# A graph-attention stage whose loads are all issued before its first group is released

## The reference, cut to what matters

```python
x = x + _L0_gnn_ref(_layernorm(x), adj, W, a)        # attention:  e = leaky_relu(s1 + s2); e = where(adj > 0, e, NEG)
                                                     #             elu(softmax(e) @ h), h = x @ W
x = x + _L0_ffn_ref(_layernorm(x), Wg, bg, W1, ...)  # 8 experts, the best two of each row, hidden size 512
x = x + _L1_gnn_ref(_layernorm(x), adj, ...)         # three steps of a GRU, each over the graph's edges
x = x + _L1_ffn_ref(_layernorm(x), gate_w, ...)      # 16 experts, the best two of each row, hidden size 256
```

## Time and profile before

| | us |
|---|---|
| median of 3 runs (1354.57 to 1358.33) | 1354.96 |
| the profiled execution, its own time | 1351.87 |
| span of its trace | 1350.0 |
| attention stage, to the first load of the experts | 274.3 |
| PE / DVE / POOL / ACT busy, whole span | 1025.9 / 797.4 / 623.2 / 563.3 |

### The profile page before, as it was taken

The page is one execution under the profiler, slowest core; times in us unless marked ns, Lnnn a source line. Parts: engine busy times, 40 slices in busy tenths (PEclk is TensorE's granted clock), DMA queues, the critical chain, the costliest instruction groups (busy, mean ns, idle before and its releaser), DMA issues. The chain is left out here.

```text
span 1350.0 us, 27968 instructions
## 1 busy us (share of the span) xinstructions
PE 1025.9 (76%) x6752; PEld 825.6 (61%) x6753; DVE 797.4 (59%) x3187; ACT 563.3 (42%) x1364; POOL 623.2 (46%) x686
## 2 busy tenths in 40 slices
PE   3666656379999999289988977979851989989930
PEld 3555445279999999245545544645430989988930
DVE  4776777445555555347767957768552444434418
ACT  3555555233333333146545644545430333333315
POOL 3577677724444554301335244253354355555540
PEclk8666666589999999789989989989965999999975
DMA  4223231222222221222203112040004322222229
GB/s 119 63 80 88 74 97 38 69 66 70 66 67 64 68 66 53 59 63 63 72 23 91 41 57 86 8 132 12 20 32 90 77 73 81 73 76 76 65 82 322
DMA packets 126205, 98.73 MB, mean 73 GB/s; under 512 B 33864, under 2 KB 115400, under 8 KB 126152
## 3 DMA queue, kind: packets, MB, share of 16 engines
q1 hardware_dynamic: 105536, 61.24, 16.7%
q0 software_dynamic: 17152, 35.29, 7.9%
q10 hardware_dynamic: 3464, 1.59, 0.6%
HBM read 55.44 MB, written 42.62 MB: 73 GB/s over the span
## 5 line engine op out<-in xcount | busy, mean ns | idle before, releaser
L1433 POOL DMA_INDIRECT result<-e_y,e_ids x280 | 274.6, 981 | 278.8 <-DVE e_y L1547 115.0
L1462 PE MATMUL e_ps_h<-e_xT,e_up_of 128*128 128x128 f32 x2240 | 290.1, 280 | 24.7 <-issue 21.8
L1462 PEld LDWEIGHTS e_ps_h<-e_xT,e_up_of 128*128 128x128 f32 x2240 | 271.4, 195 | 32.6 <-issue 29.6
L1477 PE MATMUL e_ps_y<-w_sb,e_hT 128*128 x1664 | 214.1, 278 | 5.5 <-issue 3.3
L1477 PEld LDWEIGHTS e_ps_y<-w_sb,e_hT 128*128 128x128 f32 x1664 | 200.7, 194 | 6.6 <-issue 6.2
L375 POOL DMA_INDIRECT queue<-g_q_rows,g_q_slots x128 | 129.8, 1014 | 77.9 <-DVE g_q_gap L320 38.4
L375 POOL DMA_INDIRECT queue<-a_r_rows,a_r_slots x128 | 129.0, 1008 | 63.9 <-issue 44.2
L1501 ACT ACTIVATE e_hT<-e_ps_h,b_sb 128x128 f32<-128x128 f32 x272 | 78.3, 377 | 139.6 <-remote 93.5
L1540 DVE TENSOR_SCALAR e_hT<-e_ps_h,b_sb 128x128 f32<-128x128 f32 x272 | 76.5, 343 | 84.6 <-remote 78.2
L1529 DVE COPY e_up_of<-w_sb 128x512 f32 x280 | 109.1, 430 | 5.5 <-issue 3.2
L1556 DVE TENSOR_TENSOR e_hT<-e_ps_h,e_gate 128x512 f32<-128x512 f32 x72 | 49.6, 689 | 101.7 <-ACT e_gate L1510 66.9
(11 more groups left out here) (218 smaller groups left out, 1892.4 us busy)
## 6 DMA issues: line engine op xcount, KB each, us to landing
e_xq<-queue SPq DMA_DIRECT2D x280, 64.5 KB
g_y<-result SPq DMA_DIRECT2D x16, 512.0 KB
o_y<-result SPq DMA_DIRECT2D x16, 512.0 KB, 5.3
w_sb<-w SPq DMA_DIRECT2D x48, 128.0 KB
result<-e_y,e_ids POOLq DMA_INDIRECT x280
x_res<-x SPq DMA_DIRECT2D x16, 256.0 KB
w_sb<-w SPq DMA_DIRECT2D x16, 256.0 KB
out<-x_res SPq DMA_DIRECT2D x16, 256.0 KB, 4.6
```

The costliest lines, as they stand in the source:

```text
L1433: pool.indirect_dma_start(out=result, out_offset=bass.IndirectOffsetOnAxis(ap=ids[at_down.k][:, t, :].bitcast(U32), axis=0), in_=y[at_down ...
L1462: last = pe.matmul(ps_h[b][:, t, q * P:(q + 1) * P], up_of[at_up.k % 4][:, t, q * P:(q + 1) * P], xT[at_up.k % 4][:, t, :], start=True, st ...
L1477: last = pe.matmul(ps_y[b][:, t * D:(t + 1) * D], hT[at_down.k % 4][:, t, q * P:(q + 1) * P], down[:, bass.ds(e * (chunks * P) + q * P, P) ...
```

## The change

SP issues every load of the stage in one go, without waiting for any mask: group 0, the five small weights, groups 1 to 15, the nine further weights, and each of the two expert weights as one DMA of 2 MB. For that, adj gets a buffer for all 16 groups (16 KB of each partition, in place of two buffers of 1 KB), and each group its own semaphore `arrived[s]`. When all of that is issued, SP waits for group 0's 32 counts and adds one to a new semaphore `here`, then the same for group 1, and so on to 15. DVE waits on `here` in place of `arrived`. The mask reads its group's part of the large adj buffer. Two increments of a semaphore `pad_made` and a wait on it are added around `c.pad`, since SP may now reach `pad_queues` early.

```diff
@@ gat_and_routing
-        adj_sb = [sb(f"adj{b}", [P, G, N], I32) for b in range(2)]
+        adj_sb = sb("adj", [P, NT, N], I32)
-        arrived = [sem(f"arrived{b}") for b in range(2)]
+        arrived, here = [sem(f"arrived{s}") for s in range(NG)], sem("here")
@@ sync
-            def load(at, first):
-                if not first:
-                    sp.wait_ge(arrived[at.b], 32 * at.half)
-                    alone(sp, c)
-                    wait(sp, VM, "neg", at.back(2))
-                    alone(sp, c)
-                ... (the two DMAs of group at.s)
-                if behind(at, 2):
-                    load_share(sp, weights, at.back(2), next_loaded)
-            load(At(0, 0), True)
+            def load(s):
+                sp.dma_start(c.x[:, s * G:(s + 1) * G, :], ...).then_inc(arrived[s], 16)
+                sp.dma_start(adj_sb[:, s * G:(s + 1) * G, :], ...).then_inc(arrived[s], 16)
+            load(0)
             (five small weights)
-            load(At(0, 1), True)
+            for s in range(1, NG):
+                load(s)
             (small_weights)
-            with sp.Fori(1, NG // 2) as i:
-                load(At(i, 0), False)
-                load(At(i, 1), False)
-            for s in (NG - 2, NG - 1):
-                load_share(sp, weights, s, next_loaded)
+            for dst, src in weights:
+                sp.dma_start(dst[:], src).then_inc(next_loaded, 16)
+            for s in range(NG):
+                sp.wait_ge(arrived[s], 32)
+                sp.nop(nofuse=True).then_inc(here, 1)
             sp.wait_ge(loaded, 16 * 5)
-            sp.wait_ge(next_loaded, 16 * NG * len(weights))
+            sp.wait_ge(next_loaded, 16 * len(weights))
             pad_queues(sp, c, table, c.queue0, E0, 0)
@@ vector
-                    v.wait_ge(arrived[g0.b], 32 * g0.half + 32)
+                    v.wait_ge(here, g0.s + 1)
-                    v.tensor_scalar(neg[:], adj_sb[g0.b][:], ...)
+                    v.tensor_scalar(neg[:], adj_sb[:, bass.ds(g0.s * G, G), :], ...)
@@ make_constants, pad_queues
-    pool.memset(c.pad[:, :, 0:D], 0.0)
+    pool.memset(c.pad[:, :, 0:D], 0.0).then_inc(c.pad_made, 1)
+    (the iota of c.pad increments it too, and pad_queues begins with eng.wait_ge(c.pad_made, 2))
```

More of the change, by code:

```diff
@@ L130, in program @@
         c.half_made = ctx.enter_context(nc.semaphore("half_made"))
+        c.pad_made = ctx.enter_context(nc.semaphore("pad_made"))
         c.constants_made = ctx.enter_context(nc.semaphore("constants_made"))
@@ L178, in make_constants @@
                        base=0, pattern=[[1, P]], channel_multiplier=-1).then_inc(c.constants_made, 1)
-    pool.memset(c.pad[:, :, 0:D], 0.0)
+    pool.memset(c.pad[:, :, 0:D], 0.0).then_inc(c.pad_made, 1)
     pool.iota(c.pad[:, :, D:ROW].bitcast(I32), pattern=[[P, 2 * E1], [1, 1]],
-              base=TOPK * TOKENS, channel_multiplier=1)
+              base=TOPK * TOKENS, channel_multiplier=1).then_inc(c.pad_made, 1)
 def bc(ap, n):
@@ L481, in pad_queues @@
     first = experts_n * REGION + half * per * P
+    eng.wait_ge(c.pad_made, 2)
     eng.dma_start(queue[first:first + per * P, :].rearrange("(u p) r -> p u r", p=P),
@@ L576, in _ @@
         def _(sp):
-            def load(at, first):
-                if not first:
-                    sp.wait_ge(arrived[at.b], 32 * at.half)
-                    alone(sp, c)
-                    wait(sp, VM, "neg", at.back(2))
-                    alone(sp, c)
[L584 to L588, removed]
-                if behind(at, 2):
-                    load_share(sp, weights, at.back(2), next_loaded)
-            load(At(0, 0), True)
+            def load(s):
+                sp.dma_start(c.x[:, s * G:(s + 1) * G, :],
+                             x[s * GN:(s + 1) * GN, :].rearrange("(t p) d -> p t d", p=P)).then_inc(arrived[s], 16)
+                sp.dma_start(adj_sb[:, s * G:(s + 1) * G, :],
+                             adj[s * GN:(s + 1) * GN, :].rearrange("(t p) d -> p t d", p=P)).then_inc(arrived[s], 16)
+            load(0)
             for dst, src in ((w_sb[:, 0:D], gat_w), (wT_sb[:], gat_wT), (a2_sb[:], gat_a2), (gw_sb[:], gate_w),
@@ L696, in body @@
                 if g0:
-                    v.tensor_scalar(neg[:], adj_sb[g0.b][:], 0.0, NEG, ALU.is_le, ALU.mult).then_inc(VM.sem, 1)
+                    v.tensor_scalar(neg[:], adj_sb[:, bass.ds(g0.s * G, G), :], 0.0, NEG, ALU.is_le, ALU.mult).then_inc(VM.sem, 1)
                 if g1:
```

## The result

The changed kernel takes 1377.47 us (median of 4 runs, 1373.32 to 1382.48), the kernel before, timed beside it, 1355.51. The ratio is 1.016, with an interval of 1.0119 to 1.0201: slower by about 22 us. Forecast were 1375 and 1370 to 1386. The profiled execution took 1373.32 us, 21.45 more than that of before (the sum had said 20.0).

The account below looks back on a forecast made before the run. It took POOL's indirect DMAs and the DVE, PE, ACT, DVE chain giving it slots, 14.7 us a step, as the bound. Only the late release counted: 1354.96 + 20.0 = 1375 us, range 1370 to 1386.

Parts of the forecast that it names:

- sign of being wrong: SP's last issue past 28 us, or first normalisation 20 us later without the attention stage's end being so.
- Part 1: SP's waits for masks in the attention stage go: worth nothing, since DVE never waited for a load.
- Part 2: Group 0's release moves behind all 48 SP issues (24.5 us), first normalisation from 8.68 to 28.6: +20.0 us.
- unhindered pitch: SP's issues not slowed by outstanding transfers, as when four 512 KB loads went out at 0.51 us each.
- rival B: SP's issues are held up by the transfers: +26 to +31, wholly hindered +36; 1380 to 1391 us; chance 0.27.
- Part 3: Groups 1 to 15: their data lands before it is needed, so no later wait.
- Part 4: Loop steps without their 640 KB of loads: taken as 0 gain, bounds 0 and 18.7 us.
- Rival C: Loop runs faster without loads and pays the start back: 1356 us at 1.56 a step; chance 0.04.
- Part 5: Mask address on the loop counter, `pad_made`, SP's loop gone, fewer weight DMAs: 0, at most 1 us.
- Rival D: The last 4 MB of expert weights collide with the first steps: +5 on top, 1380 us; chance 0.07.
- Rival E: SP's issues are quick with nothing between them, so no delay at the start: 1355 us; chance 0.01.
- Behind the stage everything shifts unchanged: Stages after attention: first load of the experts at 294, from there the same 1075.7 us to the end.

Follow-up runs that it names:

- direct: Changed kernel, but DVE waits for the data of groups 0 to 5 at their own semaphores, not for `here`; ratio to the kernel before 0.9985, repeated 0.9998.
- early_release: Changed kernel, but SP raises `here` for a group once the next group's loads are issued and the group has landed; ratio to the kernel before 0.9987.
- second chip: Chip on which both kernels were run again unedited: kernel before 1259.23 us, changed kernel 1286.39 us.
- wide_rows: Changed kernel with x and adj cut into rows of 2 KB and 1 KB, so values differ; ratio to the kernel before 1.0109.
- after: The changed kernel as first profiled, with no further edit: median 1377.47 us, profiled execution 1373.32 us.
- before: The kernel without the change, as first profiled: median 1355.51 us timed beside the changed kernel, profiled execution 1351.87 us.
- two_weights: Kernel before, with the expert weights as two DMAs of 2 MB behind the small weights and no shares in the loop; ratio to it 1.0013.
- weights_first: Changed kernel with the two expert weights issued before group 1 instead of last; ratio to the kernel before 1.0258.

## Why the prediction was right, and where its steps were not

The direction and the place were right: the release behind 48 issues, nothing else, makes the kernel slower (direct, early_release). That the total of 1375 came out at 1377 is in part luck: two errors partly cancel. The prediction's own sign of being wrong came true, for it named a last issue past 28, and the last issue ended at 30.92; and the stage's end moved by 14.5 where the first normalisation moved by 25.7. Where loop and later stages are alike in both kernels, on the second chip, the loss is 27 us.

*Part 1, the waits for masks: worth 0.* Right. direct takes them away and stands at 0.9985 and 0.9998.

*Part 2, +20.0.* Mis-sized: it measured +25.7, and +25.8 on the second chip. Everything around the issues held: the release came 0.16 us behind the last one (0.2 assumed), and from the statistics to the first normalisation it is 3.31 (1.63 + 1.51 = 3.14 assumed). The 24.5 us of issue were 30.1. The step that failed is the choice of the unhindered pitch, on the grounds of the 2 MB that had gone out at 0.51 each; that is rival B's mechanism, at the lower edge of its size. That row couldn't show the hold: it ends after 4 x 512 rows of 1 KB, about as many as the changed kernel had outstanding when its hold began (some 1900). Held by the transfers, the 25 loads from 7.57 on took 0.72 each in place of 0.515, which is 5.1 of the 5.6 us that were missing; where the rows are wide, 48 issues end at 23.6 (wide_rows). Rival B's own upper bound, 41, was too high by another step: 1.79 us of all engines a group was read as the time at a share of 1, but a full window shows a share of 1.22, and 1.79 / 1.22 = 1.47 is what a group takes. With that its sum is 36; the rest is that SP need not wait for all that stands ahead of it.

*Part 3, later groups don't wait.* Right; no row of after has DVE waiting for `here` a second time.

*Part 4, no gain from a loop without loads.* Right on the chip where both kernels could be compared (198.1 and 199.4 us for fifteen steps). In the first pair of profiles 11 us came back and the later stages took 7 of them, and that is why the forecast of 20 met a measured 22 instead of some 26. I can't show the cause of either. The part's reason holds even in that pair: the loop's last step in before was no shorter, though the loads had ended. Rival C needed 1.3 us a step before less than 4 us of loss was left; the twelve steps gave 14.69 - 13.57 = 1.12.

*Part 5, small edits: 0.* Right, by direct. Rival D, weights beside the first steps: at most 2 us (two_weights). Rival E, quick issues, is out: in the unbroken runs of issues at the start no two stand less than 0.43 us apart, and most 0.475. The Trainium skill (DMA: Bandwidth & Descriptors, "Issuing engines are not separate DMA queues") calls the sequencer's time usually small beside the DMA's own. These runs don't agree: in wide_rows SP's 0.475 us an issue sets the release, and a load's transfer there is hardly longer (0.393 MB in two loads at 374 GB/s, 0.53 us each); with short rows SP is held, and issue and transfer go at one pace.

*Behind the stage everything shifts unchanged.* Right on the second chip, where the rest of the span is 997.8 us before and 996.2 after; in the first pair it was 7 us longer.

## What to carry to other kernels

A semaphore that an issuing engine raises stands behind everything in that engine's list, so the first release belongs behind the first loads, however many loads follow (early_release), or the consumer waits for the loads' own semaphore (direct); both take the loss away, though neither beats the kernel before. Price a run of issues between two terms: the number of issues at 0.47 to 0.55 us is the least it takes, and the bytes ahead at the rate that their row length allows is about the most, since some of them may still be on their way. In the changed kernel the groups' last load was out at 25.5, where 37 unhindered issues would end at 19.7 and 6.43 MB at 261 GB/s take 24.6, with some 2 us before the first bytes. Loads that nobody waits for are not worth moving up front.

## What the runs showed of the hardware

- SP's issue of a DMA is held when much is outstanding: one issue took 7.23 us (weights_first), during which the DMA engines moved 2.9 MB. Bytes alone don't decide it: 4.2 MB in long rows were issued in 0.91 us, and SP was held with 0.73 MB of short rows outstanding (after) but not with 1.44 MB of wide ones (wide_rows). The number of rows, or what goes with it, has a part; the rule is open.
- Not held, SP issues one load every 0.475 us, and every 0.55 where loads of 512 rows follow each other.
- Rows of 512 and 256 bytes moved at 261 GB/s with all 16 engines full, the same bytes in rows of 2 KB and 1 KB at 374, expert weights in rows of 16 KB at 419 to 436.
- The DMA share of a full window was 0.98 to 1.06 with long rows and 1.22 to 1.24 with short ones, so a share must be divided by that of a full window of the same kind before it is used as time.
- One program took 1259 us on one chip and 1356 on another, with the experts' and GRU stages 4 to 18% longer, while the changed kernel's attention stage ended alike on both (288.85 and 288.44); a difference of a few microseconds between two traces is evidence only with a repeat on one chip.
